# Attention and mixture of experts on one core: the expert weights are split in the first expert tiles instead of in the attention steps

## What is computed

```python
h = _layernorm(x, axis=-1) * (1 + ca) + sa
x = x + ga * attention(h, W_q, W_k, W_v, W_o)      # phi = elu + 1, causal running sums
h = _layernorm(x, axis=-1) * (1 + cb) + sb
normed = _layernorm(h, rn_g, rn_b)
logits = jnp.einsum('bld,ed->ble', normed, router_w) + router_b
top_w, top_idx = jax.lax.top_k(logits, 2)          # softmax over the two
for e in range(8):
    g = _layernorm(h, ln_g[e], ln_b[e])
    g = gelu(jnp.einsum('bld,di->bli', g, w1[e]) + b1[e])
    g = jnp.einsum('bli,id->bld', g, w2[e]) + b2[e]
    out = out + combine[..., e:e + 1] * g
x = x + gb * out
```

## Time and profile before

| | us |
|---|---|
| median of 3 runs | 1143.8 (1143.52 to 1146.16) |
| the profiled execution | 1141.68 |
| its span, first to last instruction | 1139.9 |
| busy in the span: PE, DVE, POOL, ACT | 998.6, 904.4, 577.7, 541.8 |

### The profile page before, as it was taken

One profiled execution on the slowest core, in us unless ns is written; L12 is line 12 of the kernel. 1 busy time (PEld: TensorE's weight loads), 2 busy tenths in 40 slices (PEclk: granted clock), 3 DMA queues, 4 the chain that ended last, 5 costly groups with the idle time before them and its releaser, 6 DMA issues.

```text
span 1139.9 us, 31762 instructions
## 1 busy us (share of the span) xinstructions
PE 998.6 (88%) x8148; PEld 806.4 (71%) x8149; DVE 904.4 (79%) x2934; ACT 541.8 (48%) x1138; POOL 577.7 (51%) x479
## 2 busy tenths in 40 slices
PE   5668877887874499888999999999999999999996
PEld 2335545554554388777888888888888888888875
DVE  6588999999875298767788788788878878888885
ACT  2577779777833133333344434343433344344342
POOL 2112757675756535665544454455445445545542
PEclk8798889888855599999999999999999999999998
DMA  5557686967788445644434444455454445454452
GB/s 163 151 192 239 203 265 207 353 228 254 261 302 307 112 117 96 165 108 90 82 67 75 89 78 80 79 85 75 73 84 73 71 79 78 69 90 93 71 86 35
DMA packets 172394, 154.58 MB, mean 136 GB/s; under 512 B 107708, under 2 KB 154664, under 8 KB 167976
## 3 DMA queue, kind: packets, MB, share of 16 engines
q1 hardware_dynamic: 139496, 98.92, 31.3%
q0 software_dynamic: 32832, 54.88, 24.1%
HBM read 96.77 MB, written 62.78 MB: 140 GB/s over the span
## 4 chain that ended last, share of the span: by engine, by line
PE 59%; another core or an unknown queue 3%; DVE 2%; issue 2%; ACT 1%; POOLq 0%; ACTq 0%; DVEq 0%
PE banks L1449 30%; PE banks L1461 29%; ACT gf L670 1%; DVE store L1356 0%; ACT nhl L664 0%; DVE rowbuf L1347 0%; DVE store L1358 0%; DVE rowbuf L1337 0%; DVE nhl L1308 0%; POOLq L62 0%; DVE xT L1301 0%; ACT L670 0%; DVE ydst L1328 0%; DVE rowbuf L1139 0%
## 5 line engine op out<-in xcount | busy, mean ns | idle before, releaser
L1449 PE MATMUL banks<-nhl,store 128*128 128x256 bf16 (+1 forms) x3408 | 452.3, 269 | 33.2 <-ACT gf L670 22.1
L670 ACT ACTIVATE gf<-banks,b1t 128x256 f32<-128x256 f32 (+1 forms) x568 | 262.5, 464 | 454.5 <-PE banks L1449 365.0
L1461 PE MATMUL banks<-store 128*128 (+1 forms) x3240 | 449.1, 273 | 0.6 <-DVE store L1358 0.3
L610 POOL DMA_INDIRECT out<-rowbuf,ydst x135 | 216.3, 1602 | 329.9 <-DVE rowbuf L1347 210.1
L1449 PEld LDWEIGHTS banks<-nhl,store 128*128 (+1 forms) x3408 | 322.0, 98 | 83.5 <-issue 33.9
L1461 PEld LDWEIGHTS banks<-store 128*128 128x128 bf16 x3240 | 311.1, 98 | 42.7 <-issue 1.8
L1356 DVE CAST store<-gf 128x256 bf16<-128x256 f32 (+1 forms) x568 | 168.1, 296 | 117.3 <-ACT gf L670 69.2
L1358 DVE TENSOR_TENSOR store<-gf,store 128x256 bf16<-128x256 f32 (+1 forms) x568 | 234.8, 413 | 19.5
L568 POOL DMA_INDIRECT lists<-store,slot x128 | 145.8, 1139 | 92.4 <-DVE store L1072 57.4
L576 POOL DMA_INDIRECT csB<-y_rows,ygb x135 | 141.8, 1050 | 43.3 <-issue 40.0
L560 POOL TENSOR_TENSOR rs<-ve,mhalf 128x12 f32<-128x12 f32 (+2 forms) x21 | 39.5, 1880 | 79.2 <-DVE ve L828 77.2
(11 more groups left out here) (242 smaller groups left out, 1030.6 us busy)
## 6 DMA issues: line engine op xcount, KB each, us to landing
store<-wsplit SPq DMA_DIRECT2D x18, 1024.0 KB
wsplit<-store SPq DMA_DIRECT2D x16, 1024.0 KB
vk<-lists SPq DMA_DIRECT2D x256, 64.0 KB
b2t<-in_L_ffn_b SPq DMA_DIRECT2D x71, 128.0 KB
store<-in_L_attn_x SPq DMA_DIRECT2D x16, 512.0 KB
store<-in_L_ffn_w SPq DMA_DIRECT2D x32, 256.0 KB
store<-in_L_ffn_w SPq DMA_DIRECT2D x8, 1024.0 KB
out<-store SPq DMA_DIRECT2D x16, 512.0 KB
```

Source lines behind the costliest of these rows:

```text
L610: g.indirect_dma_start(out_rows, bass.IndirectOffsetOnAxis(ap=ydst[:, r, h:h + 1], axis=0), yt[:, r, h, :], None, compute_op=ALU.add).then ...
L670: a.activation(gf[:, c % 2, 0:halves(j) * P], hidden(j)[c % 2][:, 0:halves(j) * P], ACT.Gelu, bias=b1t[:, r, c:c + 1]).then_inc(gf_s, 1)
L1449: last = t.matmul(hidden(j)[c % 2][:, 0:halves(j) * P], w, nhl[:, r, m, 0:halves(j) * P], start=n == 0, stop=n == 5)
L1461: last = t.matmul(ACC[r][h][:, 0:D], g[:, c, h * P:(h + 1) * P], w, start=c == 0 and n == 0, stop=c == NI - 1 and n == 2)
```

## The change

- In attention nothing is split any more. w1 is still loaded there, for the bias alone, which PE now forms as columns (128 matmuls with one column instead of 64 with 512); ACT copies 8 columns, and the detour of the bias through device memory goes.
- The raw weights are loaded and split in the tiles: half an expert a tile, in tiles 0 to 12 and 14. Chunk 1 and chunk 4 of such a tile have one head on ACT (`head_of`) and one rest on DVE (`rest_of`) each, of 128x1024. The first expert is split in steps 17 and 18 of attention. SP's loads of raw halves (`raw_loads`, 1 MB) stand between its tile loads, and wait for the rests that free the buffer.
- Experts run in rotated order, from the fullest on, so that expert q of the order is split into place q. `table` gets a fourth row with the real numbers (`real_experts`), PE waits for the splits by a list (`READY`).
- `gf` has four buffers, and gelu of chunk c waits for the rest of chunk c - 4 instead of c - 2. The rounding on DVE is as before.
- `turn` of tiles 0 and 1 comes behind the routing of step 17, `split_rows` of both in step 19. The bias of the first five tiles is copied by DVE. DVE's first 15 tiles and ACT's first 16 are written out instead of looped.

```diff
+        def split_at(j, c):
+
+            if not isinstance(j, int) or c not in (1, 4) or j > 2 * E - 2 or j == 2 * E - 3:
+                return None
+            half = min(j, 2 * E - 3)
+            return 1 + half // 2, half % 2, c // 3
...
-        gf = sb("gf", [P, 2, TOK])
+        gf = sb("gf", [P, 4, TOK])
...
             def step(i, half, r):
...
-                    sp.wait_ge(rest1_s, NK * half + NK)
...
-                    sp.dma_start(wsplit_d[half, :, 0:4096] if isinstance(half, int) else wsplit_d[ds(half, 1), :, 0:4096],
-                                 wbuf[:, 0:4096]).then_inc(w1_out, 16)
...
+            def raw_loads(q, e, part):
+
+                if part == 0:
+                    if q == 0:
+                        sp.wait_ge(b1p_s, E)
+                    elif q < E - 1:
+                        sp.wait_ge(rest_s, 4 * q - 2)
...
+                    for n in range(4):
+                        sp.dma_start(raw_first(q)[n * 32:(n + 1) * 32, :, :], w1_v[ds(e, 1), n]).then_inc(got_a, 16)
+                else:
+                    wait_past(sp, rest_s, 4 * q if q < E - 1 else 4 * q + 2)
+                    hold(sp, "sp")
+                    sp.dma_start(raw_second(q).rearrange("p (c d) -> p c d", c=NI), w2_v[ds(e, 1)]).then_inc(got_b, 16)
...
-                wait_past(act, gl_s, NI * j + c - 1)
+                wait_past(act, gl_s, NI * j + c - 3)
...
+            def head_of(q, part, n):
...
+                if part == 0:
+                    act.wait_ge(got_a, 64 * q + 64)
+                    act.wait_ge(par_s, 1)
+                    a.activation(wall[:, q, n * I:(n + 1) * I], raw_first(q)[:, n, :], ACT.Copy, scale=par[:, q, n:n + 1]).then_inc(head_s, 1)
+                else:
+                    act.wait_ge(got_b, 16 * q + 16)
+                    a.activation(wall[:, q, 4096 + n * I:4096 + (n + 1) * I], raw_second(q)[:, n * I:(n + 1) * I], ACT.Copy).then_inc(head_s, 1)
...
-                if project and r == 1:
-
-                    act.wait_ge(got_w2e, 16 * half + 16)
-                    wait_past(act, w2_out, 16 * half)
-                    hold(act, "act")
-                    a.activation(wbuf[:, 4096:6144], w2f, ACT.Copy).then_inc(head2_s, 1)
...
-                if project and r == 1:
-
-                    dve.wait_ge(head1_s, NK * half + NK)
-                    hold(dve, "dve")
-                    for k in range(NK):
-                        v.scalar_tensor_tensor(wbuf[:, 2048 + k * 1024:2048 + (k + 1) * 1024], w1f[:, k, :], lngb[:, half, k:k + 1],
-                                               wbuf[:, k * 1024:(k + 1) * 1024], ALU.mult, ALU.subtract).then_inc(rest1_s, 1)
-                if r == 0 and (not isinstance(i, int) or 0 < i <= NB):
-
-                    dve.wait_ge(head2_s, half)
-                    hold(dve, "dve")
-                    v.tensor_tensor(wbuf[:, 6144:8192], w2f, wbuf[:, 4096:6144], ALU.subtract).then_inc(rest2_s, 1)
...
+            def rest_of(q, part, n):
+                dve.wait_ge(head_s, 4 * q + 2 * part + n + 1)
+                hold(dve, "dve")
+                if part == 0:
+                    v.scalar_tensor_tensor(wall[:, q, 2048 + n * I:2048 + (n + 1) * I], raw_first(q)[:, n, :], par[:, q, n:n + 1],
+                                           wall[:, q, n * I:(n + 1) * I], ALU.mult, ALU.subtract).then_inc(rest_s, 1)
+                else:
+                    v.tensor_tensor(wall[:, q, 6144 + n * I:6144 + (n + 1) * I], raw_second(q)[:, n * I:(n + 1) * I],
+                                    wall[:, q, 4096 + n * I:4096 + (n + 1) * I], ALU.subtract).then_inc(rest_s, 1)
...
+            READY = {EARLY + 1: 2, EARLY + 2: 3, EARLY + 4: 4, EARLY + 6: 5, EARLY + 9: 6}
```

More of the change, by code:

```diff
@@ L694, in step @@
                     act.wait_ge(b1p_s, half + 1)
[L695 to L697 removed]
+                    a.activation(b1raw[:, half, :], Q[:, 0:NI], ACT.Copy).then_inc(b1r_s, 1)
                 if project:
@@ L754, in step @@
                 if i == NB + 1:
+                    for part in range(2):
+                        for n in range(2):
+                            head_of(0, part, n)
+                if i == NB + 2:
                     for q in range(2):
@@ L769, in step @@
                     a.activation(q2[H:2 * H, r, P:T], qk[0:H, r, P:T], ACT.Copy).then_inc(q2_s, 1)
-                if project and r == 1:
-                    act.wait_ge(got_w2e, 16 * half + 16)
-                    wait_past(act, w2_out, 16 * half)
-                    hold(act, "act")
-                    a.activation(wbuf[:, 4096:6144], w2f, ACT.Copy).then_inc(head2_s, 1)
-                if project and r == 0:
-                    act.wait_ge(got_w1e, 64 * half + 64)
-                    act.wait_ge(lge_s, 1)
-                    wait_past(act, w1_out, 16 * half)
-                    hold(act, "act")
-                    for k in range(NK):
-                        a.activation(wbuf[:, k * 1024:(k + 1) * 1024], w1f[:, k, :], ACT.Copy,
-                                     scale=lngb[:, half, k:k + 1] if isinstance(half, int) else lngb[:, ds(half, 1), k:k + 1]).then_inc(head1_s, 1)
             pipeline(a, step)
-            gelu(0, 0, 0)
-            gelu(1, 0, 1)
-            with a.Fori(1, FULL // 2 - 1) as h:
+            for j in range(2 * E):
+                gelu(j, j // 2, j % 2)
+            with a.Fori(E, FULL // 2 - 1) as h:
                 for r in range(2):
@@ L893, in _ @@
             chain(v.tensor_copy(lngb[:, :, 0:2], vecs[:, VEC_G:VEC_B].rearrange("p (k e) -> p e k", k=NK)))
+            for n in range(2):
+                chain(v.tensor_copy(gains2[:, n * E:(n + 1) * E, :], vecs[:, VEC_G:VEC_B].rearrange("p (k e) -> p e k", k=NK)))
             chain(v.tensor_copy(lngb[:, :, 2:4], vecs[:, VEC_B:VEC_RG].rearrange("p (k e) -> p e k", k=NK)))
@@ L1020, in step @@
                     absent_ranks()
+                    dve.wait_ge(b1f_s, 1)
+                    for n in range(2):
+                        early_bias = v.tensor_copy(b1t[:, n, :], b1f[:, ds(early_at[0], 1), :].rearrange("p o i -> p (o i)"))
+                    early_bias.then_inc(b1e_s, 1)
+                    for n in range(2):
+                        rest_of(0, 0, n)
+                    turn(0, 0, 0)
+                    turn(1, 0, 1)
+                if i == NB + 2:
+                    for n in range(2):
+                        rest_of(0, 1, n)
             def highest(b):
@@ L1377, in _ @@
             tile(0, 0, 0, True, False)
-            for j in range(1, EARLY):
+            for j in range(1, 2 * E - 1):
                 tile(j, j // 2, j % 2, False, False)
-            with v.Fori(EARLY // 2, FULL // 2 - 2) as h:
+            with v.Fori(E - 1, FULL // 2 - 2) as h:
                 tile(2 * h + 1, h, 1, False, False)
@@ L1508, in step @@
                     hold(pe, "pe")
-                    for k in range(NK):
-                        for n in range(2):
-                            last = t.matmul(Q[n * H:n * H + 1, :], lngb[:, half, 2 + k:3 + k], w1f[:, k, n * 512:(n + 1) * 512], start=k == 0, stop=k == NK - 1)
+                    for c in range(NI):
+                        for k in range(NK):
+                            last = t.matmul(Q[:, c:c + 1], w1f[:, k, c * P:(c + 1) * P], lngb[:, half, 2 + k:3 + k], start=k == 0, stop=k == NK - 1)
                     last.then_inc(b1p_s, 1)
@@ L1630, in _ @@
             tile(EARLY + 1, (EARLY + 1) // 2, (EARLY + 1) % 2, *used_sets)
-            for j in range(EARLY + 2, EARLY + 6):
+            for j in range(EARLY + 2, 2 * E - 1):
                 used_sets = sets_from(j - 1, 2)
```

225 lines of the change are left out of this document (126 added, 99 removed).

## The result

The changed kernel takes 1157.87 us, the median of four runs (1153.77 to 1161.93); the kernel before takes 1144.76 beside it. The ratio is 1.011 (95% interval 1.007 to 1.015). So it is slower, by 13 us, where a gain of 17 was forecast, and it lies outside the range. The profiled run took 1156.55 us for a span of 1154.8, against 1139.9.

The account below looks back on a forecast made before the run. DVE was taken to bound attention and tiles 1 to 4, PE the steady tiles. Attention -33, the passage +1 and the split in the tiles +15 gave -17 us from 1143.8, so 1127 us, range 1113 to 1140.

Parts of the forecast that it names:

- the attention term: Attention steps: removing the split from DVE and ACT gains 33 us, floor 27, ceiling 38.9.
- rival 4: Attention keeps only its floor of 27 us, the rest as forecast: 1133 us, up to 1138; chance 0.10.
- The passage: From the last L1011 of attention to the tiles: +1 us, between -5 and +5.
- POOL's pause of 1.87: In the passage, POOL's pause while six 1 MB weight loads run; loads gone there, so 1.6 us given back.
- Tiles 1 to 4: Expert tiles where DVE bounds: 9.7 us of split, less 1.6 idle, plus 1 for tables: +9, range 7 to 12.
- the tables: In tiles 1 to 4, four small operations each for `real_experts`, estimated at 2 × 0.5 us.
- Tiles 5 to 12: Eight expert tiles: the split mostly fits under POOL's hold-ups; 0.6 us a tile, +5 in all.
- the hold-up: Tiles 5 to 12: ACT waits for "remote" behind POOL's pad lists, 8 waits, 20.8 us; the split fits there in quantity.
- Tile 14 and the wait: Tile 14 with its split +0.5 us; PE's wait for all splits ahead of tile 15 +0.5.
- The first sign of being wrong: Attention steps staying over 17.5 us, which would make PE or POOL's rs the bound.
- Rival 3: DVE bounds tiles 1 to 14, which cost 50 us, attention gives its floor: +28, 1171 us; chance 0.09.
- Rival 2: DVE's rests block POOL in tiles 5 to 12: +14 us, attention's gain halfway to its floor: 1144; chance 0.10.

Follow-up runs that it names:

- Runs 6: Changed kernel, with POOL waiting ahead of the two pad lists of tiles 5 to 12 until the tile's third gl: 1118.86 us, ratio 1.013 to the kernel before.
- Run 1: Changed kernel with the bias projection put back as rows of 512 columns, part of the bias left out of the result: 1137.96 us, ratio 0.997 to the kernel before.
- run 2: Kernel before with only the bias projection turned into 16 one-column products, the bias left out of the result: 1166.33 us, ratio 1.024 to the kernel before.
- run 10: Changed kernel with DVE's rests of experts 1 to 7 cut to 64 of 1024 columns, that part left out: 1139.45 us, ratio 0.995 to the kernel before.
- Runs 9: The kernel of run 8 with POOL also waiting ahead of the pad lists: 1121.88 us, ratio 0.979 to the kernel before.
- 11: Kernel before, unchanged: 1147.32 us; with POOL's wait ahead of the pad lists alone: 1135.99, ratio 0.991; run 9 repeated beside it: 1121.87, ratio 0.978.
- run 5: Changed kernel repeated unchanged on another chip: median 1125.55 us beside 1104.34 for the kernel before, ratio 1.015.
- runs 8: Changed kernel, one-column projection halved behind the transposes of every step, raw w1 read earlier into two buffers: 1133.62 us, ratio 0.989 to the kernel before.

## Why the prediction was wrong

**The step that failed** is the sentence "The 64 matmuls of L1511 with 512 columns become 128 with one; PE has 16 of 100 us free beside them, so 0". What it put at 0 cost 26 us, and attention gained 2 us instead of 33. It was wrong in three ways.
- *The count and price.* 128 products of fp32 are 256 records of 117 ns (3.73 / 32), each with a weight load of 128 columns for one column of data (the trace has 256 loads beside them): 3.73 us a step instead of 1.88. The trace of before had the price, in a row that wasn't looked up: 16 records with 8 columns at L1599 took 1.92 us, 0.12 each. The Trainium skill, TensorE: Matmul & The Clock Gate (LDWEIGHTS (loading the stationary operand)), gives the nanoseconds of a load as its columns over 1.2; an estimate by that formula is 107 ns here. The trace comes near that at full clock, and shows 218 ns a record at half (6.99 / 32).
- *The place.* The free 16 us of PE are mostly its wait for L1021. The projection does not stand in that wait but ahead of the transposes, at the head of a chain through ACT (L739, L662, L753) to the strips. A mean of free time says nothing of a place. Runs 6 and 1 together put it at 1.8 us a step over rows, 14 us in 8 steps.
- *The clock.* Behind the one-column products, and sometimes under them, PE is at 1.2 GHz (run 2). The other 12 of the 26 us belong to this and to the late signals. In run 2 no signal was late in its odd steps (hT 0.14 or 0.15 us behind the transposes), so its 25 us are PE's own time and the clock alone.

Run 1 shows what is left without this: its last L1021 ends 27 us ahead of the last L1011 of before (304.7 to 332.0; 26 against the 330.3 of the other chip). That is the floor of the attention term, 27, and not its middle, 33: in six steps, where PE is at half clock for a part, L1669 ends 14.4 to 16.5 us into the step (once 19.4), L1005 follows it by 0.04 us, and PE bounds the step, as rival 4 had it.

**What was right.** DVE had been the bound of attention and its even steps came down to 16.2 to 17.3 us (forecast 16.3 to 17). The passage: the last scatter ends 60.2 us after the last L1021 (forecast 58 to 61), and the passage gave 1.3 us where +1 was forecast, well inside its range. But one term of it was wrong: 1.6 us were given back for POOL's pause of 1.87, since the weight loads beside it would be gone. They are gone, and the pause is still there. Steady tiles take 10.5. The last L1021, the pause and the last L577 of the changed kernel, timelines of DVE and POOL:

```profile
328.38 1.64 DVE L1021 SCALAR_TENSOR_TENSOR store<-banks,rden,store 128x256 f32<-128x256 f32 x4
...
366.21 0.97 POOL L577 DMA_INDIRECT lists<-store,slot  x1 [1.88 <-issue]
...
389.29 0.96 POOL L577 DMA_INDIRECT lists<-store,slot  x1 [0.30 <-issue]
```

**What was mis-sized.** Tiles 1 to 4 were put at +9 and cost +12.0. In run 10 they lose 9.1 of this with most of the rests' width and stay 3.0 over the kernel before, of which up to 2.0 is the narrow rests that are left; so the rests cost about 11, where 9.7 less 1.6 was counted, and the 1 us for the tables fits. Tiles 5 to 12 were put at +5 and cost +6.5: not under the hold-up, where the rest at chunk 1 lies, but behind it, where the rest at chunk 4 delays L1367 by 0.8 us. Tile 14 and the wait: +1.2, forecast +1.

**The rivals.** The first sign of being wrong that was named, steps over 17.5 us, came in every second step. Rival 3 reached the right side, for a cause that was not the one at work: the tiles stayed far below its 50 us. Rival 2's trigger is in the trace (L619 at 2.47 us), its price is not: PE's first stop is 1.81 us, as before. No rival had the cause, a matmul that changed its form. The verdict turned on a term that was given one clause and no bounds.

**What stays open.** On some chips PE's signals come late while POOL issues indirect DMAs, in attention too: in the step shown, the projection ended at 214.02 by its records and ACT's copy of it, L731, started at 217.16. Runs 9 and 11 show that holding the pad lists back takes most of this out of the tiles, though the run of six stays; that the indirect DMAs are what delays the signals was argued from their place in time alone. Why a chip does it or not, and how much it cost the odd steps on the first chip (the hT there was late by 1.0 to 2.5 us in three of eight), was not settled: the one run meant for it met a chip that didn't.

## What to carry to other kernels

Price a matmul by its records and its weights, not by its data: turning one row product into many one-column ones costs a weight load for each, and here it cost the clock of what followed. Ask of a changed instruction where it stands in the chain, since free time of its engine elsewhere covers nothing; the same products cost 25 us ahead of the transposes, and no more than their row form behind them, once the weights were read early (last L1021 at 304.9 and 304.7, on two chips). And if an engine goes on only after a run of indirect DMAs on POOL, try them in another place of the step; then look at the trace for what the edit did to their order.

## What was not expected of the hardware

- PE's granted clock fell from 1.00 to 0.50 while PE was busy without a pause: under one-column products in run 2 (186.9 to 191.2 us, 4.30 of 4.30 us busy, mean clock 0.84, then 0.50), and in run 5 under L1669, from where it stayed at 0.50 through 7.00 of 7.00 us of one-column products.
- Completions of PE's matmuls seemed to reach ACT up to 3.1 us late (L731 at 217.16 us) while POOL sent indirect DMAs. On the chip with the faster kernel before they came in time: ACT's hT started 0.15 us after the transposes in every step of run 5.
- To hold the pad lists back until the third chunk of the next tile was worth 11 us to both kernels, on the chip of runs 8 to 11.
